# A two-layer graph network on one core: q kept in the space of x, expanded by two one-hot products for each tile of edges

## The reference, cut to what matters

```
k, q, v = typed_linear(x, Wk / Wq / Wv, ntype)        # (N, 8, 16) each
a = (typed_rel(k[src], rel_att, etype) * q[dst]).sum(-1) * rel_pri.T[etype] / 4
ex = exp(a - segment_max(a, dst)[dst])
h = segment_sum(typed_rel(v[src], rel_msg, etype) * ex / den[dst], dst)
y = layernorm(x + h @ Wa[ntype] * gate + x * (1 - gate))
```

## Time and profile before

| | |
|---|---|
| time, median of 3 runs | 4505.61 us (4501.09 to 4509.4) |
| profiled execution | 4512.08 us, span 4510.3 us |
| busy: PE, PEld, DVE, ACT, POOL | 3479.3, 2387.8, 2379.0, 900.6, 2626.3 us |
| granted TensorE clock, mean | 0.863 |
| DMA | 1041.17 MB, 231 GB/s over the span |

### The profile page before, as it was taken

One profiled execution on the slowest core, in us unless ns is written; L12 is line 12 of the kernel. 1 busy time (PEld: TensorE's weight loads), 2 busy tenths in 40 slices (PEclk: granted clock), 3 DMA queues, 4 the chain that ended last, 5 costly groups with the idle time before them and its releaser, 6 DMA issues.

```text
span 4510.3 us, 56344 instructions
## 1 busy us (share of the span) xinstructions
PE 3479.3 (77%) x16302; PEld 2387.8 (53%) x16302; DVE 2379.0 (53%) x7762; ACT 900.6 (20%) x2048; POOL 2626.3 (58%) x2767
## 2 busy tenths in 40 slices
PE   2688856666666666663099999969999978999993
PEld 2577755666665565651055555545555545555552
DVE  2333336667777777774245544455544444554446
ACT  0111124555555555531100000000000000000001
POOL 0000036556777777777447677746777764767772
PEclk8799977777877777777599999979999989999996
DMA  7777757776555555420168788858788867878881
GB/s 261 271 312 305 298 187 272 269 272 198 159 143 157 146 151 152 144 71 1 65 240 299 288 297 302 300 173 308 293 294 296 302 232 256 295 289 297 296 295 49
DMA packets 367669, 1041.17 MB, mean 231 GB/s; under 512 B 77923, under 2 KB 250264, under 8 KB 324610
## 3 DMA queue, kind: packets, MB, share of 16 engines
q1 hardware_dynamic: 251090, 660.52, 40.7%
q0 software_dynamic: 108112, 321.99, 21.2%
q10 hardware_dynamic: 8160, 55.05, 3.2%
HBM read 808.64 MB, written 228.66 MB: 230 GB/s over the span
## 4 chain that ended last, share of the span: by engine, by line
PE 45%; DVE 3%; POOL 1%; issue 1%; DMA 0%; ACT 0%; POOLq 0%; DVEq 0%
PE bank L997 36%; PE bank L969 7%; POOL stage L523 1%; PE bank L1002 1%; DVE nodes L1535 1%; DVE sums L1534 1%; DVE xr L1463 0%; DVE sums L1465 0%; DVE xr L1556 0%; PE bank L981 0%; DMA stage<-h_tab,earr 0%; DVE nodes L1553 0%; DVE sums L1550 0%; PE bank L1015 0%; DVE sums L1503 0%
## 5 line engine op out<-in xcount | busy, mean ns | idle before, releaser
L523 POOL DMA_INDIRECT stage<-h_tab,earr x1536 | 1452.7, 946 | 778.3 <-issue 361.9
L997 PE MATMUL bank<-arena,xr 128*128 128x512 f32 (+1 forms) x3822 | 1693.9, 590 | 9.1 <-DVE xr L1463 9.1
L997 PEld LDWEIGHTS bank<-arena,xr 128*128 128x128 f32 x3822 | 697.8, 191 | 722.2 <-issue 712.6
L1503 DVE TENSOR_TENSOR sums<-sums,bank 128x128 f32 x1536 | 435.6, 284 | 781.1 <-PE bank L969 776.3
L500 POOL DMA_INDIRECT arena<-kv_tab,idxr x560 | 539.9, 964 | 301.7 <-issue 167.8
L1474 DVE TENSOR_SCALAR oh<-iota_j,earr 128x128 f32<-128x128 f32 x1536 | 586.7, 385 | 90.6 <-DVE sums L1494 43.1
L969 PEld LDWEIGHTS bank<-oh,stage 128*128 128x128 f32 x3072 | 408.9, 196 | 236.1 <-issue 190.3
L969 PE MATMUL bank<-oh,stage 128*128 128x128 f32 x3072 | 421.5, 282 | 51.8 <-DMA stage<-h_tab,earr 41.8
L665 ACT ACTIVATE rs<-mv,epsc 128x49 f32<-128x49 f32 (+1 forms) x6 | 1.9, 317 | 2241.2 <-DVE mv L1537 2015.4
L838 PE MATMUL bank<-arena 128*128 128x128 f32 x1664 | 255.9, 310 | 190.1 <-issue 99.1
L481 POOL DMA_INDIRECT a_tab<-tot,cell x320 | 320.9, 1003 | 100.2 <-issue 100.2
(11 more groups left out here) (216 smaller groups left out, 3228.4 us busy)
## 6 DMA issues: line engine op xcount, KB each, us to landing
arena<-a_tab SPq DMA_DIRECT2D x273, 1792.0 KB
a_tab<-sums POOLq DMA_DIRECT2D x61, 1792.0 KB, 9.3
a_tab<-arena ACTq DMA_DIRECT2D x30, 1792.0 KB
arena<-q_tab SPq DMA_DIRECT2D x832, 64.0 KB
...
arena<-rel_d SPq DMA_DIRECT2D x52, 512.0 KB, 5.0
...
```

Of the source, the lines that this page charges most:

```text
L523: G.indirect_dma_start(gring[:, (q % NG) * GRP + s, :], None, h_tab[l], bass.IndirectOffsetOnAxis(src_i[:, t:t + 1], 0)).then_inc(row_land ...
L997: mm = M.matmul(o_[:, 0:cw], xr[:, n, :], abuf[B % NBUF][:, n % KB, 0:cw], start=n == 0, stop=n == NT - 1)
L1503: V.tensor_tensor(w_, w_, bank[q % NG][:, s * P:(s + 1) * P], ALU.add).then_inc(win_added, 1)
```

## The change

1. q is not stored to HBM. `copy_qkv` writes the q rows of node tile n over x in `xr[:, n, :]`, and x is loaded again after the last `q_rows` (two DMAs). `q_tab` and its 832 loads of 64 KB are gone.
2. Relative destinations now count from the start of a node tile. Each `q_rows` reads from SBUF: four registers are loaded on TensorE (`load_blocks`), and each edge tile takes two products, with node tiles `block` and `block + 1`. `one_hot_T` makes two one-hots, so two Abs and two Relu for each group. The start of the node tile is worked out in `edge_group` (seven more small instructions in each of seven groups), stored to `blk_d` and loaded once.
3. The totals of equal pairs are made on VectorE alone, by one `scalar_tensor_tensor` with a running sum for each edge tile, eight for each node tile, at the end of `table(n)`. Its inputs, the keys and the weights, are loaded by SP to all 128 partitions, 512 KB each, in three buffers.
4. Zeros: GpSimd writes 31 blocks instead of 61, the first at once and each next one with the progress of the tables. The other 60 are on SP's queue in `feed`, two for each batch from 1 to 30, 3.5 KB to a descriptor instead of 7 KB.
5. Scatters: eight for each batch from SB = 32 (160), then 48, then the addition to x, and then the last 112.
6. The third gather buffer moves from `xr` to the arena.

```diff
-SB = 17
+KT = 8
+KR = 3
+SB = 32
+SPB = 8
+SY = 48
 ZB = 2
...
-        kv.append(xr[:, 0:2 * TPB, :].rearrange("p n f -> p (n f)").rearrange("p (t f) -> p t f", t=TPB))
+        late = arena[:, at - part_words(sizes[7:]):at]
+        kv.append(late[:, 0:TPB * 2 * D].rearrange("p (t f) -> p t f", t=TPB))
...
+        kew = big[:, 0:KR * 2 * KT * P].rearrange("p (a k e) -> p a k e", a=KR, k=2)
...
-        eq = qwin[:, 2 * GRP:4 * GRP, :].rearrange("p (a s) e -> p a s e", a=2)
-        relw = qwin[:, 0:2 * GRP, :].rearrange("p a f -> p (a f)").bitcast(BF16).rearrange("p (a e) -> p a e", a=16)
+        same = prep[:, 2 * GRP:2 * GRP + KT, :]
...
-        at = sum(n for _, n in sizes[0:5])
-        zero = arena[:, at:at + KB * 256]
-        ZT = 61
+        ZW = KB * 512 // 4
+        zero = stage[:, :, :, :].rearrange("p a r f -> p (a r f)")[:, TPB * P:TPB * P + ZW]
+        ZT = 31
...
+                                 ro[0:n, 2 + g % 2, 0, :]).then_inc(edge_saved[g % 2], 16)
...
+                if c == 0:
+                    sp.wait_ge(edge_rows, EG)
+                    sp.wait_ge(edge_cols, EG)
+                    for a in range(2):
+                        sp.wait_ge(edge_saved[a], edges_saved(a, EG))
+                    sp.dma_start(base_row[32:33, :], blk_d[0:ET].rearrange("(a t) -> a t", a=1)).then_inc(blk_in, 16)
+                if c >= KR:
+                    sp.wait_ge(tot_added, KT * (c - KR + 1))
+                for k, rows in enumerate((key_d, ew)):
+                    sp.dma_start(kew[:, c % KR, k, :], rows[c * KT * P:(c + 1) * KT * P].rearrange("(a e) -> a e", a=1)
+                                 .to_broadcast([P, KT * P])).then_inc(kew_in[c % KR], 16)
...
-                sp.dma_start(q_tab[bass.ds(n * P, P), :], qkv[:, par, 0, :]).then_inc(q_saved[par], 16)
...
+                for c in ((0, 1) if n == QSTEP - 1 else (n - QSTEP + 2,)):
+                    if 0 <= c < KC and n >= QSTEP - 1:
+                        load_keys(c)
...
-                    sp.wait_ge(ohT_ready, NG * (b - 1))
+                    sp.wait_ge(ohT_ready, 2 * NG * (b - 1))
...
-                for g in range(NG):
-                    firsts = load_starts(mybir.EngineType.SP, b * TPB + g * GRP)
-                    if g == 2 and not peeled:
-                        sp.wait_ge(logit_turned, b)
-                    elif not (b == 0):
-                        sp.wait_ge(q_done, NG * (b - 1) + g + 1)
-                    for s in range(GRP):
-                        sp.dma_start(qwin[:, g * GRP + s, :], q_tab[bass.ds(firsts[s], P), :]).then_inc(qwin_in[g], 16)
-                    if g == 2:
-                        sp.dma_start(negs[:, par, 0, :], negf_d[bass.ds(b * P, P), :]).then_inc(neg_in[par], 16)
-                        sp.dma_start(negs[:, par, 1, :], negb_d[bass.ds(b * P, P), :]).then_inc(neg_in[par], 16)
+                if not peeled:
+                    sp.wait_ge(logit_turned, b)
+                sp.dma_start(negs[:, par, 0, :], negf_d[bass.ds(b * P, P), :]).then_inc(neg_in[par], 16)
+                sp.dma_start(negs[:, par, 1, :], negb_d[bass.ds(b * P, P), :]).then_inc(neg_in[par], 16)
+                if b == 1:
+                    sp.wait_ge(zero_set, 2)
+                if b >= 1:
+                    for z in range(ZT + ZB * (b - 1), min(NBLK, ZT + ZB * b)):
+                        sp.dma_start(a_flat[z, :, :].rearrange("p (a f) -> p a f", a=4),
+                                     zero.rearrange("p (a f) -> p a f", a=1).to_broadcast([P, 4, ZW])).then_inc(a_rest_zeroed, 16)
...
-            sp.wait_ge(vw_ready, NG * (max(b for b in range(NB) if b % 3 == 2) + 1))
-            sp.dma_start(xr[:, 0:2 * TPB, :], x[0:2 * TPB * P, :].rearrange("(i p) f -> p i f", p=P)).then_inc(x_in, 16)
+            sp.wait_ge(q_done, NG * NB)
+            sp.dma_start(xr[:, 0:NF, :], x[0:NF * P, :].rearrange("(i p) f -> p i f", p=P)).then_inc(x_in, 16)
...
-                if b > 6:
-                    pool.wait_ge(kv_copied, 4 * (b - 6) // 5)
+                if b:
+                    pool.wait_ge(kv_copied, b * NT // ZT)
...
-                        scatter(NG * (b - SB) + g)
+                        for k in range(SPB // NG):
+                            scatter(SPB * (b - SB) + k * NG + g)
...
-            for t in range(NG * (NB - SB), T1):
+            for t in range(SPB * (NB - SB), min(T1, SPB * (NB - SB) + SY)):
                 scatter(t)
             pool.wait_ge(y_set, 1)
             G.tensor_tensor(xr[:, :, :], xr[:, :, :], lnw[:, 1:2, :].to_broadcast([P, NT, D]), ALU.add).then_inc(xb_ready, 1)
+            for t in range(SPB * (NB - SB) + SY, T1):
+                scatter(t)
...
-                S.activation(qkv[:, par, :, :], bank[2][:, 0:3 * D].rearrange("p (k f) -> p k f", k=3), ACT.Copy)\
+                S.activation(xr[:, n, :], bank[2][:, 0:D], ACT.Copy).then_inc(q_ready, 1)
+                S.activation(qkv[:, par, :, :], bank[2][:, D:3 * D].rearrange("p (k f) -> p k f", k=2), ACT.Copy)\
...
-                al.link(S.activation(ohT[:, g % 2, :], relb[:, par, g * GRP * P:(g + 1) * GRP * P], ACT.Abs, scale=-1.0,
-                                     bias=iota_p[:, 0:1]))
-                S.activation(ohT[:, g % 2, :], ohT[:, g % 2, :], ACT.Relu, scale=-1.0, bias=epsc[:, 1:2]).then_inc(ohT_ready, 1)
+                for k in range(2):
+                    al.inc(S.activation(ohT[k][:, g % 2, :], relb[:, par, g * GRP * P:(g + 1) * GRP * P], ACT.Abs, scale=-1.0,
+                                        bias=iota_p[:, k:k + 1]))
+                for k in range(2):
+                    al.wait(1 - k)
+                    S.activation(ohT[k][:, g % 2, :], ohT[k][:, g % 2, :], ACT.Relu, scale=-1.0, bias=epsc[:, 1:2])\
+                     .then_inc(ohT_ready, 1)
...
-                al.at((TPB + NG) * (b - 1) + NG + 2)
-                for z in range(ZT + ZB * (b - 1), min(NBLK, ZT + ZB * b)):
-                    act.dma_start(a_flat[z, :, :].rearrange("p (a f) -> p a f", a=2),
-                                  zero.rearrange("p (a f) -> p a f", a=1).to_broadcast([P, 2, KB * 256]))\
-                       .then_inc(a_rest_zeroed, 16)
...
-            def turn_keys(q):
-                pe.wait_ge(key_ready, GRP * q // P + 1)
-                pe.wait_ge(edge_cols, EG)
-                if q:
-                    pe.wait_ge(eq_ready, q)
-                for s in range(GRP):
-                    last = M.transpose(bank[7][:, s * P:(s + 1) * P],
...
-                pe.wait_ge(eq_ready, q + 1)
-                if q >= 2:
-                    pe.wait_ge(tot_added, q - 1)
-                else:
-                    pe.wait_ge(cell_ready, 1)
-                for s in range(GRP):
-                    last = M.matmul(bank[1 + 2 * (q % 2)][:, s:s + 1], eq[:, q % 2, s, :], ew_c[:, GRP * q + s:GRP * q + s + 1],
-                                    start=True, stop=True)
-                last.then_inc(tot_done, 1)
...
             def table(n, par):
-                qs = key_quads(n)
                 if n + 2 < NT:
                     turn(n + 2, par)
-                if key_quads(n - 1):
-                    sum_keys(key_quads(n - 1)[1])
-                if qs:
-                    turn_keys(qs[0])
                 if n + 1 < NT:
                     project(n + 1, 1 - par)
-                if qs:
-                    sum_keys(qs[0])
-                    turn_keys(qs[1])
                 relate(n, par)
...
+                blocks = load_blocks(mybir.EngineType.PE, b * TPB + g * GRP)
+                pe.wait_ge(ohT_ready, 2 * (NG * b + g + 1))
                 if not (NG * b + g < 2):
                     pe.wait_ge(logit_done, NG * b + g - 1)
                 for s in range(GRP):
-                    last = M.matmul(bank[g % 2][:, s * D:(s + 1) * D], ohT[:, g % 2, s * P:(s + 1) * P],
-                                    qwin[:, g * GRP + s, :], start=True, stop=True)
+                    for k in range(2):
+                        last = M.matmul(bank[g % 2][:, s * D:(s + 1) * D], ohT[k][:, g % 2, s * P:(s + 1) * P],
+                                        xr[:, k:NT - 1 + k, :][:, bass.ds(blocks[s], 1), :].rearrange("p a f -> p (a f)"),
+                                        start=k == 0, stop=k == 1)
...
-            def match_keys(q):
-                dve.wait_ge(key_turned, q + 1)
-                if q >= 2:
-                    dve.wait_ge(tot_done, q - 1)
-                V.tensor_tensor(eq[:, q % 2, :, :], bank[7][:, :].rearrange("p (s e) -> p s e", s=GRP),
-                                key[:, GRP * q:GRP * (q + 1)].rearrange("p (s a) -> p s a", a=1).to_broadcast([P, GRP, P]),
-                                ALU.is_equal).then_inc(eq_ready, 1)
-            def add_totals(q):
-                dve.wait_ge(tot_done, q + 1)
-                V.tensor_copy(tot[:, GRP * q:GRP * (q + 1)], bank[1 + 2 * (q % 2)][:, 0:GRP]).then_inc(tot_added, 1)
+            def add_totals(c):
```

(32 more changed lines are left out.)

98 lines of the change are left out of this document (49 added, 49 removed).

## The result

The changed kernel takes 4407.26 us in the median of 4 runs (4405.8 to 4408.99), the kernel before beside it 4507.5 us (4501.09 to 4511.32): a ratio of 0.9779, 95% interval 0.9762 to 0.9796. That is 100 us less where 35 were predicted (4471 us, range 4375 to 4580). Direction and range hold, the size does not. The profiled execution has a span of 4406.8 us, 103.5 us less than before.

A forecast was written before the change was run, and what follows sets the result against it. Bounds: TensorE in stage 1, late q windows then GpSimd's scatters in stage 2, GpSimd alone between the stages. Terms -30 + 65 + 22 - 92 = -35 us gave 4477 us profiled, 4471 us median; range 4375 to 4580 us.

The forecast's parts named there:

- the five terms: The kernel's time split by stage boundaries, predicted at -30, +65, +22, -104 and +12 us.
- rival (b): Stage 1: TensorE keeps its fast clock level, tiles give -39 us instead of +65; 4367 us, chance 0.25.
- rival (c): Stage 2: register loads and ScalarE's second pair of instructions make a batch 27.5 us; 4573 us, chance 0.17.
- Tiles with totals, +65 us: Stage 1: VectorE's eight sums lengthen the loop to 11.7 us a tile, 40 tiles 468 us against 403.
- The sentence on the accumulator: VectorE's sums in stage 1: each counts as two instructions, so the stage is 20 to 35 us later than summed.
- Edge tiles, -30: First tiles of stage 1: no burst of zeros ahead of stores saves 38 us, 8 us given back.
- A batch without scatters, 24.1 us: Stage 2: 20.5 us plus doubled q_rows products and 0.7 us for register loads; bounds 21.5 and 27.5 us.
- Stage 2, +22: Gather batches: 27 + 30 x 24.1 + 608 us for 20 batches with scatters, 1357 us against 1336.
- Between the stages, -92: Last gather to first dense product: addition ahead of 112 scatters, 104 us earlier, 12 us given back.
- (d): Stage 2: the relb row for the one-hots lands late behind zeros, 5 us a batch; 4621 us, chance 0.10.
- (e): Gap between the stages stays: addition held up or gathers late, -40 instead of -92; 4523 us, chance 0.06.
- (a): Whole kernel: the forecast itself, 4471 us, own range 4418 to 4522 us, chance 0.42.

The follow-up runs named there:

- e2: Changed kernel with each of the eight sums of a tile made twice; 13.65 us from mask to mask.
- e14: Changed kernel with the eight sums ahead of the copies of k and v instead of behind them; 4352.27 us, 0.9651 of the kernel before.
- e3: Changed kernel with the first nine blocks of zeros issued at once again; mask of tile 9 at 199.2 us, 19.1 later.
- e11: Kernel before with its zeros issued with the progress of the tables, none at once; 0.9960 of the kernel before, some 20 us.
- e8: Changed kernel without the second product of each pair; where every kernel took a fifth longer, most batches 34.6 us instead of 37.6.
- e4: Kernel before with only the order of the last scatters changed (48, addition to x, then 132); 0.9948 of the kernel before.
- e12: Changed kernel with all 160 last scatters ahead of the addition to x again; 1.0257 of the kernel before.

## Why the prediction was right and where it failed

The direction came from the right places, edge tiles and the gap between the stages. The size did not: measured less predicted, the five terms are off by +7, -59, -20, +11 and -8 us. The time lies in the range because the range was 205 us wide, made to reach from rival (b) to rival (c), not because the sum was near.

**The step that failed is "Tiles with totals, +65 us": measured +6.0.** The loop was the right one (copy, sums, mask, products, in the timeline and by e2), and the sums nearly so: 2.18 us instead of 2.5. What was mis-sized is the rest of the tile. I took the 9.2 us of tile 8, "products at the slow level", for a tile that would idle "over 3 us". That row stood behind 7.96 us of idle time (timeline of the kernel before); the new tiles idle 2.7 us, and their rest costs 8.07 us.

```profile
194.28 1.12 PE L768 MATMUL bank<-ident,arena 128*128 128x128 f32 x4 [7.96 <-DVE arena L1136]
```

The runs e2 and e14 show the scale at both ends: 9.25 us behind 5.0 us, 6.44 us behind 0.5 us. So 10.25 us a tile and not 11.7: over 37 tiles from mask to mask that is 54 us of the 59 missing. The others are of both signs: tiles 9 and 10 took 15.5 and 10.8 us, 6 us more than 10.25 each, since VectorE waited 6.8 us for tile 9's weights; and the sum counted 40 tiles though the last ones mask nothing and overlap, 11 us less. Rival (b), with chance 0.25, was half of the truth: 2.65 us for the 16 records, between 3.4 and 1.95.

**The sentence on the accumulator.** The Trainium skill, VectorE: DVE Perf Modes, "Two Vector instructions with no wait between them", makes such a sum two instructions. The trace agrees (347 and 82 ns), but the second runs within the first of the next pair: 0.27 us for each pair, so the stage did not come later by it.

**Edge tiles, -30: measured -22.7.** The burst was the cause (e3, e11) and is worth 19 to 30 us. "I give back 8 us for stores that are still waited for" was too little: 22.2 us of waits are left, and e11 shows 22.3 us of such waits in the kernel before too, once the burst is gone. New small instructions: 7.8 us for seven groups, 1.1 each where 1.4 were counted.

**A batch without scatters, 24.1 us: measured 23.4.** Three times 0.9 us of products are in the timeline as counted, and e8, in a long session, gives 2.6 us. "0.7 us that is not covered by products" for registers isn't there: `q_rows` follows `aggregate` without idle time. 20.5 + 2.9 = 23.4. That is the second step that failed: a cost was counted that did not occur. **Stage 2, +22: measured +1.8.** Up to the first scatter at 1325.7 us it was 28 us ahead of the sum, 21 of them by 30 times 0.7 us; the 480 DMAs from there to T took 615 us instead of 608.

**Between the stages, -92: measured -88.6** with what stage 3 gave back. The addition came at T + 68 (66 predicted), the end of scatters at T + 230 (221), VectorE's chain at T + 209 (205), the dense product 6.9 us behind the first block's load (6), and 4.4 us came back in stage 3 instead of 12. The term is right in the profile of the changed kernel. Its cause, the order, is argued there from what released what; e4 and e12 confirm it in direction alone, in sessions where another chain ends last.

**The rivals.** (c), a late loop with 27.5 us, did not occur: no gaps ahead of `q_rows`, ScalarE 79% busy. (d): behind zeros `relb` lands 16.0 us after its issue and without them 4.5 us, so it does stand behind zeros, but inside the 19 us that it had, and ScalarE waits 1 us. The Trainium skill, DMA: Bandwidth & Descriptors, "Queues, rings and completion order", has descriptors taken in ring order on each DMA engine; the trace agrees, with a delay of 11.5 us. That is near the 12 us of two blocks at 291 GB/s and far from two landings of 9.3. (e) did not occur.

**A sum in the prediction.** Its own range for (a), 4418 to 4522 us, is said to add two spreads "as independent ones do"; that gives 4421 to 4513 us. Neither holds the 4407 us, and nothing else hangs on it.
